# Residual biases of three projections: from a product on TensorE to an addition on GpSimd

## The reference

```
x = x + window_attention(norm(x)) @ Wo0.T + bo0             # tag a
x = x + (masked_attention(norm(x), ctx) @ Wp.T + bp) * mask # tag b
x = x + slot_ffn(norm(x))                                   # tag f
x = x + causal_attention(norm(x)) @ Wproj + bproj           # tag 1
x = x + cross_attention(norm(x), ctx) @ Wo.T + bo           # tag x
x = x + ternary_conv_ffn(norm(x))                           # tag g
```

## Time and profile before

| | |
|---|---|
| time, median of 3 runs | 3288.36 us (3285.29 to 3289.53) |
| the profiled execution's own time | 3283.83 us |
| its span, first to last instruction | 3282.0 us |
| mean granted TensorE clock | 0.955 of full speed |
| setup, up to the last setup instruction of VectorE | about 67 us |
| one turn of the repeating part | about 386 us |

### The profile page before, as it was taken

How to read it: one execution, slowest core, us unless ns; L and a number is a source line. 1 busy time by engine, 2 the same in 40 slices (tenths; PEclk the granted TensorE clock), 3 DMA queues, 4 the chain that set the end, 5 groups by cost and what they waited for, 6 DMA issues and landing times.

```text
span 3282.0 us, 59801 instructions
## 1 busy us (share of the span) xinstructions
PE 2836.4 (86%) x23406; PEld 2073.9 (63%) x23406; DVE 2522.0 (77%) x5446; ACT 2178.7 (66%) x4271; POOL 755.3 (23%) x1360
## 2 busy tenths in 40 slices
PE   3799986999878998899988998889988999889985
PEld 3566754676656766577666676567665676656763
DVE  6856599766898579975898769986799768987676
ACT  2368764678646876577855777657865687557773
POOL 1420013300233112330133112422032301232100
PEclk8799997999989999899999999999999999999996
DMA  5000010000000000000000000000000000000000
GB/s 157 1 1 1 4 27 17 1 1 5 24 12 9 1 16 12 20 1 1 16 21 11 1 4 13 24 9 1 5 24 12 9 1 16 16 17 1 1 1 13
DMA packets 43468, 43.47 MB, mean 13 GB/s; under 512 B 8577, under 2 KB 41185, under 8 KB 43185
## 3 DMA queue, kind: packets, MB, share of 16 engines
q1 hardware_dynamic: 41200, 36.46, 3.8%
q10 hardware_dynamic: 1984, 3.18, 0.3%
HBM read 31.24 MB, written 8.39 MB: 12 GB/s over the span
## 4 chain that ended last, share of the span: by engine, by line
PE 49%; DVE 31%; ACT 11%; POOL 4%; issue 4%; DMA 1%; SPq 0%; DVEq 0%; POOLq 0%; ACTq 0%
PE banks L1179 8%; PE banks L1213 7%; DVE chain_m L696 5%; PE banks L1322 4%; PE banks L1222 4%; PE banks L1260 4%; PE banks L1197 3%; DVE chain_arena L890 3%; PE banks L1286 2%; DVE chain_arena L927 2%; PE banks L1406 2%; DVE chain_arena L730 2%; DVE chain_arena L931 2%; DVE chain_stat L674 2%; DVE chain_arena L774 2%
## 5 line engine op out<-in xcount | busy, mean ns | idle before, releaser
L1213 PE MATMUL banks<-chain_arena 64*128 64x256 f32 x3072 | 426.2, 399 | 42.4 <-DVE chain_m L696 28.1
L696 DVE TENSOR_REDUCE chain_m<-banks 128x4 f32<-128x512 f32 x512 | 328.7, 681 | 84.8 <-PE banks L1213 84.2
L1515 POOL TENSOR_SCALAR chain_ng<-chain_sv 128x2 f32<-128x2 f32 x192 | 52.9, 276 | 1408.4 <-DVE chain_sv L677 1408.3
L1213 PEld LDWEIGHTS banks<-chain_arena 64*128 64x128 f32 x3072 | 286.0, 191 | 119.9 <-DVE chain_m L696 41.2
L1034 ACT ACTIVATE chain_arena<-chain_arena,chain_m 128x128 f32<-128x128 f32 x1024 | 324.1, 393 | 25.9 <-DVE chain_m L696 23.2
L968 ACT ACTIVATE chain_xn<-chain_xa,chain_nm,chain_rs 128x256 f32<-128x256 f32 x384 | 209.4, 596 | 166.3 <-POOL chain_nm L1519 165.5
L1260 PE MATMUL banks<-chain_arena 64*128 64x256 f32 x2048 | 268.2, 382 | 0.0
L692 DVE TENSOR_TENSOR chain_arena<-banks,pos_bias 128x512 f32<-128x512 f32 x256 | 174.9, 683 | 95.6 <-PE banks L1213 94.6
L1222 PE MATMUL banks<-chain_arena,chain_va 128*32 128x128 f32 x5120 | 198.1, 281 | 40.5 <-ACT chain_arena L1013 27.4
L1260 PEld LDWEIGHTS banks<-chain_arena 64*128 64x128 f32 x2048 | 200.5, 192 | 23.5
L1569 POOL TENSOR_TENSOR chain_arena<-chain_arena 128x512 f32<-128x512 f32 x128 | 169.5, 1341 | 148.4 <-DVE chain_arena L774 148.0
(11 more groups left out here) (314 smaller groups left out, 6979.1 us busy)
## 6 DMA issues: line engine op xcount, KB each, us to landing
chain_xn<-in_ctx SPq DMA_DIRECT2D x32, 256.0 KB, 2.8
chain_xa<-in_x SPq DMA_DIRECT2D x32, 256.0 KB, 3.1
out<-chain_xa SPq DMA_DIRECT2D x32, 256.0 KB, 2.2
chain_arena<-in_mask SPq DMA_DIRECT2D x32, 128.0 KB, 3.5
f_w1t<-in_w1t ACTq DMA_DIRECT2D x1, 1024.0 KB, 7.0
f_w2t<-in_w2t ACTq DMA_DIRECT2D x1, 1024.0 KB, 14.3
wqkv0T<-in_wqkv0T ACTq DMA_DIRECT2D x1, 768.0 KB, 16.8
whh<-in_whh SPq DMA_DIRECT2D x1, 768.0 KB, 10.3
```

Source lines behind the costliest of these rows:

```text
L696: e.tensor_reduce(m, s.rearrange("p (j o) t -> p j o t", o=2), AX.X, ALU.max, negate=True).then_inc(*done(f"{tag}_mx{u}"))
L1213: mm[i] = e.matmul(c.ps[:, i, 2 * T * j:2 * T * j + 2 * T], t["qh"][p, j, x, b, :], flat(t["kx"][p, j, b]), start=not masked, stop=not mas ...
```

## The change

The three biases are no longer multiplied in. The setup loads each as a full tile of 128 equal rows, adds the projected value bias to two of them, and stops there. In each turn GpSimd adds the bias to `xa` in place, in a new step that comes after `xn` has been read from `xa` and that the final addition waits for. That is one 128x512 instruction per branch a, 1 and x, 96 in all. GpSimd's string grows from 544 to 640 digits; with the new steps taken out it is the old string. TensorE's string is unchanged. In VectorE's string 11 of 2720 digits differ, in ScalarE's 9 of 2592, most of them in the first turns. The four selecting matrices become two, each with the rows of two groups: a product that reads one half of one finds the same rows in it as before.

```
-    for i, name in ((0, "bo0"), (2, "bproj"), (3, "box")):
-        e.dma_start(k["bias_rows"][32 * i:32 * i + 32, :], rows(inp[name], 32)).then_inc(ld["bias_rows"], 16)
+    for i, name in enumerate(("bo0", "bproj", "box")):
+        e.dma_start(k["res_bias"][:, i, :], rows(inp[name])).then_inc(ld["bias_rows"], 16)
...
-    e.memset(k["bias_rows"][32:64, :], 0.0).then_inc(*done("no_bias"))
...
-    for i in range(GROUPS):
+    for i in range(2):
         e.tensor_scalar(k["pick"][:, i, :], k["ones"][:], k["rows_of"][:, i:i + 1], None, ALU.mult)
...
-    for i, tag in ((2, "1"), (3, "x")):
-        p = slice(32 * i, 32 * i + 32)
+    for i, tag in ((1, "1"), (2, "x")):
         e.wait_ge(*pe("bw" + tag))
-        e.tensor_tensor(rest[p, :], rest[p, :], ps[p, i, 0:D], ALU.add).then_inc(*done("bias" + tag))
-    e.wait_ge(*dve("biasx"))
-    for i in range(3):
-        e.tensor_copy(k["bias3"][:], rest[:]).then_inc(*done(f"bias_r{i}"))
...
-    e.wait_ge(*dve("bias_m2"))
-    e.tensor_copy(k["bias3"][:], part[:, 0, :]).then_inc(*done("bias3"))
+        e.tensor_tensor(k["res_bias"][:, i, :], k["res_bias"][:, i, :], ps[:, 1 + i, 0:D], ALU.add)
...
     e.wait_ge(*pe(f"{tag}_pr"))
-    if scaled:
-        e.wait_ge(*pool("b_xb"))
+    e.wait_ge(*pool(f"{tag}_xb"))
     e.tensor_tensor(flat(t["xa"][:]), c.ps[:, 1, :], flat(t["xa"][:]), ALU.add).then_inc(*done(f"{tag}_y"))
...
     e.wait_ge(*pe("a_pr"))
+    e.wait_ge(*pool("a_xb"))
     e.tensor_tensor(flat(t["xa"][:]), c.ps[:, 1, :], flat(t["xa"][:]), ALU.add).then_inc(*done("a_y"))
...
-            e.matmul(ps[:, i, :], k["pick"][p, 2 * i + o, :], flat(t["mT"][p, b]), start=True, stop=False)
+            e.matmul(ps[:, i, :], k["pick"][p, o, :], flat(t["mT"][p, b]), start=True, stop=False)
...
-def project_tensor(e, c, src, w, k, bias):
+def project_tensor(e, c, src, w):
-    if bias is not None:
-        e.matmul(c.ps[:, 1, :], k["pick"][:, bias, :], spread(k["bias3"][:], 1, B), start=True, stop=False)
     for b in range(B):
         for j in range(KT):
-            mm = e.matmul(c.ps[:, 1, D * b:D * b + D], src[:, j, b, :], w[:, j, :], start=bias is None and j == 0,
-                          stop=j == KT - 1 and (bias is None or b == B - 1))
+            mm = e.matmul(c.ps[:, 1, D * b:D * b + D], src[:, j, b, :], w[:, j, :], start=(j == 0), stop=(j == KT - 1))
...
+def bias_pool(e, c, n, tag, k, i):
+
+    e.wait_ge(*c.act.of(n)(f"{tag}_xn{B - 1}"))
+    e.tensor_tensor(c.t["xa"][:], c.t["xa"][:], spread(k["res_bias"][:, i, :], 1, B), ALU.add).then_inc(*c.pool.now(f"{tag}_xb"))
+    yield
...
     yield from norm_pool(e, c, n, "a", k)
+    yield from bias_pool(e, c, n, "a", k, 0)
...
     yield from norm_pool(e, c, n, "1", k)
+    yield from bias_pool(e, c, n, "1", k, 1)
     yield from norm_pool(e, c, n, "x", k)
+    yield from bias_pool(e, c, n, "x", k, 2)
...
-        "rows_of": np.stack([(p // 32 == i) & (p % 32 < 3) for i in range(GROUPS)] + [p % 64 == 0], 1).astype(f),
-        "third": np.stack([p % 32 == i for i in range(3)], 1).astype(f),
+        "rows_of": np.stack([(p // 32 % 2 == o) & (p % 32 < 3) for o in range(2)] + [p % 64 == 0], 1).astype(f),
```

More of the change, by code:

```diff
@@ L60 @@
     "pool": """
-        c_mk c_m2 a_pad c_va c_mask a_ng a_rs a_nm a_qk3 a_ac1 a_ac3 a_ac4 a_ac5 b_ng b_rs b_nm b_mb0 b_xb0 b_mb1
-        b_xb b_m1 b_d1 b_m2 b_m3 f_ng f_rs f_nm 1_ng 1_rs 1_nm x_ng x_rs x_nm x_m1 x_d1 x_m2 x_m3 g_ng g_rs g_nm
-        g_pad""".split(),
+        c_mk c_m2 a_pad c_va c_mask a_ng a_rs a_nm a_xb a_qk3 a_ac1 a_ac3 a_ac4 a_ac5 b_ng b_rs b_nm b_mb0 b_xb0
+        b_mb1 b_xb b_m1 b_d1 b_m2 b_m3 f_ng f_rs f_nm 1_ng 1_rs 1_nm 1_xb x_ng x_rs x_nm x_xb x_m1 x_d1 x_m2 x_m3
+        g_ng g_rs g_nm g_pad""".split(),
     "setup_dve": """
-        wd_zero ones no_bias rel pos_max wd0 wd1 wd2 wd3 c2 bvw0 bvw1 bw10 bw11 bwx0 bwx1 slots c4 c5 c6 w1t_abs
-        w1t_mean w1t_rec w1t_round w1t_min w1t c8 c9 c10 c_cw pos_eps pos_rec rel_norm c11 w2t_abs w2t_mean w2t_rec
-        w2t_round w2t_min w2t c13 c14 c15 conn_d slot_mean slotT fire_b0 fire_b1 fire_b2 fire_b3 gate_b half_hn wvo
-        bvo bias1 biasx bias_r0 bias_p0 bias_s0 bias_r1 bias_p1 bias_s1 bias_r2 bias_p2 bias_m0 bias_m1 bias_m2
-        bias3 tau inv_tau""".split(),
+        wd_zero ones rel pos_max wd0 wd1 wd2 wd3 c2 bvw0 bvw1 bw10 bw11 bwx0 bwx1 slots c4 c5 c6 w1t_abs w1t_mean
+        w1t_rec w1t_round w1t_min w1t c8 c9 c10 c_cw pos_eps pos_rec rel_norm c11 w2t_abs w2t_mean w2t_rec w2t_round
+        w2t_min w2t c13 c14 c15 conn_d slot_mean slotT fire_b0 fire_b1 fire_b2 fire_b3 gate_b half_hn wvo bvo tau
+        inv_tau""".split(),
     "dve": """
@@ L216 @@
 PACK = (("parity", 2), ("half", 2), ("conv_w", 3 * HT), ("conv_b", HT))
-NARROW = (("rows_of", 5), ("third", 3), ("bq1_c", KT), ("bk1_c", KT), ("bv1_c", KT), ("bqx_c", KT), ("bkx_c", KT), ("bvx_c", KT),
+NARROW = (("rows_of", 3), ("bq1_c", KT), ("bk1_c", KT), ("bv1_c", KT), ("bqx_c", KT), ("bkx_c", KT), ("bvx_c", KT),
           ("b1f", 1), ("bvf", KT), ("fw1", 1), ("fb1", 1), ("fw2", H), ("keys", 32))
@@ L246, in constants @@
         ("expand_bf", [96, 4, 128], BF16), ("ident_bf", [128, 128], BF16), ("ones", [128, 128], F32),
-        ("first", [128, 128], BF16), ("pick", [128, GROUPS, 128], BF16), ("neg_half", [128, B], F32), ("rounder", [128, 1], F32), ("bias3", [128, D], BF16),
+        ("first", [128, 128], BF16), ("pick", [128, 2, 128], BF16), ("neg_half", [128, B], F32), ("rounder", [128, 1], F32), ("res_bias", [128, 3, D], F32),
         ("bq1", [128, KT, 2], F32), ("bk1", [128, KT, 2], F32), ("bqx", [128, KT, 2], F32), ("bkx", [128, KT, 2], F32),
@@ L342, in setup_vector @@
     e.wait_ge(*dve("ones"))
-    for i in range(GROUPS):
+    for i in range(2):
         e.tensor_scalar(k["pick"][:, i, :], k["ones"][:], k["rows_of"][:, i:i + 1], None, ALU.mult)
-    e.tensor_scalar(k["first"][:], k["ones"][:], k["rows_of"][:, GROUPS:GROUPS + 1], None, ALU.mult)
+    e.tensor_scalar(k["first"][:], k["ones"][:], k["rows_of"][:, 2:3], None, ALU.mult)
     e.wait_ge(ld["pack"], 16)
@@ L1293, in causal_tensor, with outputs_tensor @@
         yield
-def outputs_tensor(e, c, n, tag, k, w, bias=None):
+def outputs_tensor(e, c, n, tag, k, w):
     t, ps, act, dve, done = c.t, c.ps, c.act.of(n), c.dve.of(n), c.pe.now
@@ L1374, in window_tensor @@
     e.wait_ge(*dve("a_oT"))
-    project_tensor(e, c, t["ring"][:, 3], k["wo0T"], k, 0).then_inc(*done("a_pr"))
+    project_tensor(e, c, t["ring"][:, 3], k["wo0T"]).then_inc(*done("a_pr"))
     yield
@@ L1499, in tensor_turn @@
     yield from causal_tensor(e, c, n, "1", k)
-    yield from outputs_tensor(e, c, n, "1", k, k["wproj"], 2)
+    yield from outputs_tensor(e, c, n, "1", k, k["wproj"])
     yield from flipped_tensor(e, c, n, "x", k, 0)
@@ L1504, in tensor_turn @@
     yield from softmax_tensor(e, c, n, "x", k)
-    yield from outputs_tensor(e, c, n, "x", k, k["woxT"], 3)
+    yield from outputs_tensor(e, c, n, "x", k, k["woxT"])
     yield from mlp_tensor(e, c, n, k)
```

46 lines of the change are left out of this document (17 added, 29 removed).

## The result

The changed kernel takes 3306.5 us (median of 4 runs, 3302.8 to 3309.4), the kernel before 3288.9 (4 runs on the same chip). The ratio is 1.0053, 95% interval 1.0036 to 1.0071: slower by 17.6 us. The forecast was 3292 us and no measurable change; the time also ends 0.5 us above the range.

A forecast was written before the change was run, and what follows sets the result against it. PE was taken to bound one half of a turn, DVE the other. -4.5 - 10 + 3 + 14 + 1.5 = +4 on 3283.8 us, plus 4.6 to the median: 3292; forecast's own range 3283 to 3295, whole range 3274 to 3306.

The forecast's parts named there:

- setup: End of the setup: the split of the biases goes, and its 4.5 us are saved in full.
- PE's products: 96 bias products go; 51 on the chain that ended last give back 0.21 us each, taken as 10 us saved.
- first turn: POOL's queue in the first turn: new additions ahead of the norms of chains 1 and 2 delay PE, plus 3 us.
- meetings: POOL additions stretch DVE instructions with two SBUF inputs at three places in each of seven turns: plus 14 us, bounds 0 and 19.
- D: Among chain 1's sums on POOL: two new additions delay DVE work that PE wants, 0.3 us for five turns, plus 1.5.
- PE gives back nothing: Rival: removing the bias products saves PE no time, giving 3302 us; it shares the 0.31 of the slower two.
- place A: DVE half, second of two L931: stretched 0.97 us if POOL gets in between, nothing if DVE goes through; half counted, 0.5.
- B: DVE half, L935 starting at 1678.78 beside a POOL addition: stretched by 0.97 us a turn.
- C: DVE half, L927 starting at 1733.08 beside a POOL addition: stretched by 0.82 us a turn.
- The new wait: The final addition's wait for the new POOL step: it ends last nowhere and by itself costs nothing.
- The slower rival: SBUF lock paid in full at three places in seven turns (19 us), PE giving 6: 3305 us; slower two together 0.31.

The follow-up runs named there:

- experiment 4: The kernel before with the setup's split of the biases into three bf16 parts replaced by one cast, all products kept: ratio 0.9988, 4 us less.
- experiment 1: The kernel before with its 96 bias products left out and nothing in their place: 3282.2 against 3286.7 us.
- experiment 2: The changed kernel with each of the 96 additions cut to two columns of each sequence: 3276.6 against 3286.7 us, ratio 0.9971.
- experiment 7: The changed kernel with each addition replaced by memsets of about the same POOL time that read nothing from SBUF: 3272.7 against 3287.6 us, ratio 0.9954.
- 9: The changed kernel, complete, with additions moved or held by waits on VectorE events so that they meet no instruction they hold up: 3280.2 against 3286.8 us.
- experiment 8: The kernel before with each of its 96 bias products made twice: 3296.8 against 3287.6 us, ratio 1.0026.

## Why the prediction was wrong

The three large terms, beside what the runs made of them:

| term | predicted | measured |
|---|---|---|
| setup | -4.5 | -4 (experiment 4) |
| PE's products | -10 | -5 (experiment 1) |
| additions: first turn, meetings, D | +3 +14 +1.5 | +27, 21 to 33 (changed kernel less experiment 2) |
| sum | +4 | +18; the changed kernel itself +17.6 |

**Setup.** Right, by its own rows.

**PE's products.** A size that was wrong by half, and a step that failed: that a product on the chain which ended last gives back its 0.21 us. The chain tells what was last, not by how much. At the place shown above ACT stood 0.2 us behind, and taking twelve products out of a turn changed nothing in it; the other places were not looked at one by one. What experiment 1 gave lies outside the repeating turns. The text had "PE gives back nothing" among the rivals.

**DVE beside POOL.** The mechanism was right, shown by experiments 2, 7 and 9. Its size was not: 14 us in the prediction, and most of 27 in the runs. Two steps failed. The first is the price of place A, "if DVE goes through, nothing ... I count half, 0.5": POOL got in between the two taps in each of the seven turns, and the tap took 1.0 us more. The second is that a meeting costs its own stretch, times 0.9, and nothing behind it. Moving A's addition gave 2.7 us a turn, of which its own rows hold 1.1; the rest came as waits for TensorE at a lower granted clock and as other instructions held up, for which the prediction had no term. B (0.97 predicted, 0.8 given) and C (0.82 and 0.5) came out near their price, as far as single executions tell.

The Trainium skill's rule (SBUF — State Buffer, section "SBUF: two separate sides": whoever starts first keeps the pair of ports for the whole instruction) would have had A at its full 0.97, a turn of 2.76, and the three in all 19. The trace agrees with it at A: POOL's addition took 0.2 us more, through the first tap, and then held the second. The bound of 19 was still too low, for the second reason.

The prediction also stopped at three places that repeat. Up to the end of turn 2 the changed kernel's additions hold up seven instructions, five of them at other places than A, B and C (one is a cast, L888, 1.61 us in place of 0.68). And POOL's steps behind an addition meet others than before: at A the displaced L1548 makes one L709 longer by 1.0 and leaves an L907 0.94 shorter.

**POOL's queue.** First turn: 3 predicted; the lateness is there, 1.61 and 1.07 us of PE waiting in place of the 2.0 and 1.2 worked out from the earlier trace rows:

```profile
85.46 0.93 PE L1150 MATMUL banks<-ident,chain_xn 128*128 128x128 f32 x4 [1.61 <-ACT chain_xn L948]
...
90.92 0.93 PE L1150 MATMUL banks<-ident,chain_xn 128*128 128x128 f32 x4 [1.07 <-ACT chain_xn L948]
```

But experiment 7, with the same queue and no lock, has only 0.7 us of it left at the turn's end, so the prediction read the waits of PE rightly and went wrong in adding them to the time in full. Place D: 1.5 us in all predicted, 0.2 a turn; in experiment 7 the turn's surplus is 0.4 with everything that the queue does in it. Right.

**The new wait.** No instruction waited for an addition; right. PE's busy time fell by 15 us where 39 were forecast from the products' records, which overlap with what follows them.

**The slower rival.** The lock at its full price said 3305 us, with -6 for PE and 3 + 19 + 5 = 27 for the additions. Both totals came out nearly so (-5 and 27), but partly by luck, since the parts are others: D and the first turn cost next to nothing, A more than its stretch. A small slip stands in it: by the prediction's own terms the forecast's range ends where the meetings cost 16.6 us (3295 is 2.6 over 3292.4), not 18.

**What stays open.** In their profiled executions experiments 2, 4 and 9 are 9, 5 and 10 us ahead of before at the end of turn 0, and lose 7, 4 and 11 us of it in turns 1 to 3, though no addition of 9 holds anything up, those of 2 are short and 4 has none. The granted clock differs there: 0.944 as the mean of these three turns for 2 and 9, against 0.957 before. But 4 has the same 0.957 (0.919 against 0.931 in turn 1, where it loses 4 us), and experiment 7, with 0.918 in turn 1, loses only 0.6 us there. So the clock may take a part of it, and no run shows how much.

## What to carry to other kernels

Work that moves to an idle GpSimd was free here only at moments at which VectorE had no instruction with two inputs in SBUF (or a cast from SBUF, below). So look for the partner first: put the GpSimd instruction beside reductions or operations on PSUM, hold it there with a wait on VectorE's own event if need be, and check that the GpSimd steps behind it don't move into a meeting. The same 96 additions cost 27 us where they came by themselves and about 2 where they were placed. A piece on the chain that ended last is worth no more than the distance to what stands behind it, whatever its length: taking 0.21 us off twelve places of a turn gave nothing in the turn. And a delay can cost more than its own length: before you price one, look at the granted clock and at the partners of the instructions behind it.

## What the runs showed of the hardware

- POOL got in between two DVE instructions of the same kind that stand back to back: at A its addition started during the first and took 1.46 in place of 1.27 us, and the second was held, 1.92 us for the pair against 0.89 before.
- A POOL memset of 1.14 us in the same place holds nothing up (0.90 us for the pair). The Trainium skill's page (SBUF — State Buffer, same section) says that two SBUF inputs of DVE collide only with a GpSimd instruction that reads SBUF; experiment 7 agrees.
- An instruction with a single SBUF input was held too, one that casts float32 to bf16: L873 takes 0.41 us where nothing is in its way. In experiment 1 it started while POOL's sums ran (POOL, then DVE), and took 1.58. The trace of before has such a meeting at 1335.88 us (1.57), and L888, another cast, shows it above. The prediction had looked for pairs of inputs only.

```profile
2108.08 2.49 POOL L1568 TENSOR_TENSOR chain_arena<-chain_arena 128x512 f32<-128x512 f32 x2
...
2109.28 1.58 DVE L873 TENSOR_SCALAR chain_arena<-chain_xn 128x512 bf16<-128x512 f32 x1
```

- The same eight float32 products of a projection took 2.57 us where the granted clock was 0.83 over 10 us, and 3.51 us where it was 0.66 (experiment 8, lines of PE for the windows shown there):

```profile
2038.89 2.57 PE L1322 MATMUL banks<-woxT,chain_arena 128*128 128x256 f32 x8
...
2049.13 3.51 PE L1323 MATMUL banks<-woxT,chain_arena 128*128 128x256 f32 x8
```
